# A recurrent attention block with a routed expert layer: VectorE's own reciprocal, two jobs moved from GpSimd to ScalarE, an earlier first set of masked queries, and zero products in the prologue

## The reference

```python
Z1 = xk @ W1_s + b1_s
grad = _ln_fused_l2_bwd(Z1, xv - xk, ln_w, ln_b)
Attn1 = jnp.tril(xq @ xk.swapaxes(-1, -2))
Z1_bar = xq @ W1_s - eta_mb * Attn1 @ grad + b1_bar
W1_new = W1_s - (last_eta * xk).swapaxes(-1, -2) @ grad
out = xq + _ln(Z1_bar, ln_w, ln_b)
```

## Time and profile before

| what | value |
|---|---|
| median of 3 runs | 233.45 us (232.33 to 238.2) |
| the profiled execution, its own time | 233.13 us |
| its span, first to last instruction | 231.2 us, so 1.93 us lie around it |
| VectorE busy | 198.5 us (86%) |
| TensorE busy, matmuls | 194.6 us (84%) |
| GpSimd busy | 154.4 us (67%) |
| ScalarE busy | 115.7 us (50%) |
| mean granted TensorE clock | 0.938 |

### The profile page before, as it was taken

The page is one execution under the profiler, slowest core; times in us unless marked ns, Lnnn a source line. Parts: engine busy times, 40 slices in busy tenths (PEclk is TensorE's granted clock), DMA queues, the critical chain, the costliest instruction groups (busy, mean ns, idle before and its releaser), DMA issues.

```text
span 231.2 us, 5305 instructions
## 1 busy us (share of the span) xinstructions
PE 194.6 (84%) x1893; PEld 154.4 (67%) x1893; DVE 198.5 (86%) x525; ACT 115.7 (50%) x235; POOL 154.4 (67%) x212
## 2 busy tenths in 40 slices
PE   8533999778789979889999985999799599998772
PEld 6313567256678768677968873879588488866551
DVE  2899999999995999999999999999999999206962
ACT  2462179553529063736555755157564556147230
POOL 2314539897779458597687649769999977464234
PEclk9975899979999979999999999799999799988998
DMA  5995200217613000374120044103000300400022
GB/s 166 374 405 169 75 4 0 71 37 157 204 12 91 3 0 10 91 119 65 27 73 3 0 100 135 48 10 91 0 3 10 93 3 0 145 40 0 3 91 91
DMA packets 26000, 17.44 MB, mean 75 GB/s; under 512 B 10552, under 2 KB 24312, under 8 KB 25464
## 3 DMA queue, kind: packets, MB, share of 16 engines
q1 hardware_dynamic: 25464, 16.25, 25.2%
q10 hardware_dynamic: 512, 0.87, 1.2%
HBM read 15.22 MB, written 1.87 MB: 74 GB/s over the span
## 4 chain that ended last, share of the span: by engine, by line
DVE 38%; PE 34%; ACT 8%; POOL 8%; issue 7%; DMA 2%; POOLq 0%; SPq 0%; DVEq 0%; ACTq 0%
PE bank L1174 9%; PE bank L1215 7%; PE bank L1187 5%; PE bank L1133 5%; DVE pr L821 4%; DVE bank L832 4%; DVE pr L880 4%; DVE dW L885 3%; PE bank L1201 3%; POOL hT L355 2%; POOL gw L350 2%; DMA small<-in_small 2%; POOL sgpad L374 2%; PE bank L1251 2%; PE bank L1109 1%
## 5 line engine op out<-in xcount | busy, mean ns | idle before, releaser
L1174 PE MATMUL bank<-xn_hi,gup_hi 128*128 128x256 f32 x128 | 41.0, 320 | 1.6 <-ACT up L583 1.6
L1187 PE MATMUL bank<-down,hT 128*128 128x256 f32 x128 | 34.4, 393 | 4.5 <-ACT G L587 2.5
L350 POOL TENSOR_TENSOR gw<-gate,share 128x256 f32<-128x256 f32 x32 | 23.4, 730 | 21.5 <-ACT gate L582 21.0
L1174 PE MATMUL bank<-xn_hi,gup_lo 128*128 128x256 f32 x128 | 36.9, 288 | 0.0
L1174 PE MATMUL bank<-xn_lo,gup_hi 128*128 128x256 f32 x128 | 36.9, 288 | 0.0
L290 POOL TENSOR_TENSOR A<-A,mask 128x256 f32<-128x256 f32 x32 | 23.5, 735 | 13.2 <-ACT A L565 13.2
L1174 PEld LDWEIGHTS bank<-xn_hi,gup_hi 128*128 128x128 f32 x128 | 25.1, 196 | 7.6 <-issue 4.2
L1187 PEld LDWEIGHTS bank<-down,hT 128*128 128x128 f32 x128 | 22.9, 198 | 7.1 <-issue 2.7
L565 ACT ACTIVATE A<-bank,one 128x256 f32<-128x256 f32 x32 | 15.0, 469 | 23.2 <-PE bank L1133 23.2
L1174 PEld LDWEIGHTS bank<-xn_hi,gup_lo 128*128 128x128 f32 x128 | 25.2, 197 | 0.2
L355 POOL TENSOR_TENSOR hT<-gw,up 128x256 f32<-128x256 f32 x32 | 23.4, 730 | 2.9 <-PE bank L1187 0.5
(11 more groups left out here) (158 smaller groups left out, 436.7 us busy)
## 6 DMA issues: line engine op xcount, KB each, us to landing
wblk<-w_blocks SPq DMA_DIRECT2D x8, 512.0 KB, 4.0
share<-shares SPq DMA_DIRECT2D x8, 512.0 KB, 8.3
sgpad<-in_gup SPq DMA_DIRECT2D x1, 1024.0 KB, 9.6
G<-in_gup SPq DMA_DIRECT2D x1, 1024.0 KB, 11.7
down<-in_down SPq DMA_DIRECT2D x1, 1024.0 KB, 14.2
xkT<-in_x_bt SPq DMA_DIRECT2D x1, 1024.0 KB, 4.8
out<-G SPq DMA_DIRECT2D x4, 256.0 KB, 2.5
wkv<-in_wkv ACTq DMA_DIRECT2D x1, 512.0 KB, 4.2
```

The lines of the kernel that those rows point to most:

```text
L350: pool.tensor_tensor(gw[:, :], gate[:, i % 2, :], share[:, pair % 2, e, :], ALU.mult).then_inc(S_["gw"], 1)
L1174: ins = pe.matmul(bank[4 + i % 2][:, 2 * P * g:2 * P * g + 2 * P], w[:, k, e, NI * g:NI * g + NI].bitcast(F32R), x[:, k, 2 * pair:2 * pair ...
L1187: ins = pe.matmul(bank[7][:, HS * r:HS * r + HS], hT[:, i % 2, P * r:P * r + P], down[:, e, :], start=(e == 0 and r == 0), stop=(e == NE - ...
```

## The change

1. **VectorE and ScalarE, each minibatch.** The sum of squares is taken over 9 columns per token instead of 8; the ninth holds 8*eps, set once. So sxx is 8*(v + eps) with no bias. VectorE takes the reciprocal of sxx itself (16 values, no wait for ScalarE) and multiplies it by ScalarE's square root (16 values) to get the other row. ScalarE's second row (L572) is gone, and its square root has no bias operand. The factor 8 is taken up by constants elsewhere; the last addition to x becomes one operation with a factor 1/8.
2. **Masked queries** go from GpSimd to ScalarE (four `Copy` activations with a per-partition scale): those of group 0 behind the second sigmoid and the sqrt table, of group 1 behind `query_rows(1)`, of group j + 1 behind `step_std(2j+2)` and ahead of the group's remaining slots.
3. **Keys by token** of groups 3 to 7 go from GpSimd to ScalarE, behind `step_std(2j+1)`.
4. **ScalarE's prologue**: the copies of xn's channels (groups 1 to 3) go ahead of `input_std(2)`.
5. **TensorE's prologue**: 2, 7 and 1 zero products.

The core of the diff:

```diff
-        T = sb("T", [P, 5, HD * K])
+        T = sb("T", [P, 4, HD * K])
+        XX = sb("XX", [P, K, HD + 1])
...
-                act.activation(sv[:, 0, :], sxx[:, :], ACT.Sqrt, bias=eps[:, 0:1], scale=1.0 / HD).then_inc(S_["rstd"], 1)
-                act.activation(sv[:, 1, :], sxx[:, :], ACT.Identity, bias=eps[:, 0:1], scale=1.0 / HD).then_inc(S_["rstd"], 1)
+                act.activation(sv[:, :], sxx[:, :], ACT.Sqrt, scale=1.0 / HD).then_inc(S_["rstd"], 1)
...
+            link(v.memset(XX[:, :, HD:], HD * EPS))
...
-                v.tensor_reduce(sxx[:, :], xx, AX.X, ALU.add).then_inc(S_["vrc"], 1)
+                v.tensor_reduce(sxx[:, :], XX[:, :, :], AX.X, ALU.add).then_inc(S_["vrc"], 1)
...
-                v.wait_ge(S_["rstd"], 2 * n + 2)
-                v.reciprocal(rr, sv[:, :, :]).then_inc(chain, 1)
+                v.wait_ge(S_["vrc"], n + 1)
+                v.reciprocal(rr[:, 1, :], sxx[:, :]).then_inc(chain, 1)
+                v.wait_ge(S_["rstd"], n + 1)
+                done(9)
+                v.tensor_tensor(rr[:, 0, :], rr[:, 1, :], sv[:, :], ALU.mult).then_inc(chain, 1)
...
-                v.tensor_tensor(x, x, b3(cs[:, 0, :]), ALU.add).then_inc(S_["sg"], 1)
+                v.scalar_tensor_tensor(out=x, in0=b3(cs[:, 0, :]), scalar=1.0 / HD, in1=x,
+                                       op0=ALU.mult, op1=ALU.add).then_inc(S_["sg"], 1)
...
+            def masked_queries(j):
+
+                act.wait_ge(S_["qchc"], 2 + 2 * (j // 4))
+                if j >= 2:
+                    act.wait_ge(S_["sc"], 4 * (j - 1))
+                for h in range(4):
+                    act.activation(xqm[:, j % 2, :, :, h, :], xqT[:, :, :, GT * j:GT * j + GT], ACT.Copy,
+                                   scale=cmask[:, h:h + 1]).then_inc(S_["queries"], 1)
+
+            def keys_by_token(j):
+
+                act.wait_ge(S_["pair_done"], j)
+                act.copy(KT[:, j % 2, :, 0:HD], KP[:, j % 2, 0:HD, :].rearrange("p c t -> p t c")).then_inc(S_["kts"], 1)
...
-            input_std(2, 4, 8)
             xn_out((2, 4), 2, 1, 4)
+            input_std(2, 4, 8)
...
+            masked_queries(0)
             step_std(2)
...
             query_rows(1)
+            masked_queries(1)
...
+                    if j < NG - 1:
+                        keys_by_token(j + 1)
                     scores_out(j, 2)
...
                     step_std(2 * j + 2)
                 if j == 4:
                     scores_out(j, 4)
+                if j < NG - 1:
+                    masked_queries(j + 1)
                 for i in slots:
                     expert_slot(i)
...
+            zero_products(2)
             pe.wait_ge(S_["wt"], 1)
             target_rows(0, bank[5][:, 0:256]).then_inc(S_["pair0"], 1)
+            zero_products(7)
             xn_channels((2, 4), 1, 4)
+            zero_products(1)
```

More of the change, by code:

```diff
@@ L128, in build @@
         sxx = sb("sxx", [P, K])
-        sv = sb("sv", [P, 2, K])
+        sv = sb("sv", [P, K])
         cs = sb("cs", [P, 2, K])
@@ L327, in bias_targets @@
                 pool.wait_ge(S_["pair_done"] if j else S_["pair0T"], j or 1)
-                if j:
+                if j in (1, 2):
                     pool.tensor_copy(KT[:, j % 2, :, 0:HD], KP[:, j % 2, 0:HD, :].rearrange("p c t -> p t c")).then_inc(S_["kts"], 1)
@@ L331, in bias_targets @@
                 pool.tensor_tensor(q, q, gb[:, :].unsqueeze(1).broadcast_to([P, GT, HD]), ALU.add).then_inc(S_["targets"], 1)
-            def masked_queries(j):
-                pool.wait_ge(S_["qchc"], 2 + 2 * (j // 4))
-                if j >= 2:
-                    pool.wait_ge(S_["sc"], 4 * (j - 1))
-                for h in range(4):
-                    pool.tensor_scalar(xqm[:, j % 2, :, :, h, :], xqT[:, :, :, GT * j:GT * j + GT],
-                                       cmask[:, h:h + 1], 0.0, ALU.mult, ALU.add).then_inc(S_["queries"], 1)
             def hidden_product(i):
@@ L505, in input_std @@
                 if n == 0:
-                    act.wait_ge(S_["dve0"], 3)
+                    act.wait_ge(S_["dve0"], 4)
                 act.activation(std_in[:, first:end], mv[:, first:end, 1], ACT.Sqrt,
@@ L632, in _ @@
             step_std(0)
+            xn_out((2, 4), 2, 1, 4)
             input_std(2, 4, 8)
-            xn_out((2, 4), 2, 1, 4)
             keys_out(0, (0, 1), 0, 4)
@@ L648, in _ @@
             preload_sqrt(1)
+            act.wait_ge(S_["small2"], 16)
+            masked_queries(0)
             step_std(2)
@@ L797, in route_choices @@
                                     mif[:, :, k:k + 1].broadcast_to([P, NF, NE]), ALU.is_equal).then_inc(S_["onehot"], 1)
-            OPS = 17
+            OPS = 18
             def minibatch(j, ring, m, fill, last=False):
@@ L812, in minibatch @@
                 b3 = lambda a: a.unsqueeze(2).broadcast_to([P, K, HD])
-                xs, xx, u, pq, ux = (td(T[:, i, :]) for i in range(5))
+                xs, u, pq, ux = (td(T[:, i, :]) for i in range(4))
                 x = td(x_ps)
@@ L841, in minibatch @@
                 done(3)
-                v.tensor_tensor(xx, x, xs, ALU.mult).then_inc(chain, 1)
+                v.tensor_tensor(XX[:, :, 0:HD], x, xs, ALU.mult).then_inc(chain, 1)
                 done(4)
@@ L845, in minibatch @@
                 done(6)
-                v.tensor_reduce(sxx[:, :], xx, AX.X, ALU.add).then_inc(S_["vrc"], 1)
+                v.tensor_reduce(sxx[:, :], XX[:, :, :], AX.X, ALU.add).then_inc(S_["vrc"], 1)
                 done(7)
-                v.tensor_reduce(S[:, :, :], T[:, 2:5, :].rearrange("p k (t d) -> p k t d", d=HD), AX.X,
+                v.tensor_reduce(S[:, :, :], T[:, 1:4, :].rearrange("p k (t d) -> p k t d", d=HD), AX.X,
                                 ALU.add).then_inc(chain, 1)
                 fill(1)
-                v.wait_ge(S_["rstd"], 2 * n + 2)
-                v.reciprocal(rr, sv[:, :, :]).then_inc(chain, 1)
+                v.wait_ge(S_["vrc"], n + 1)
[3 more added lines that the diff above has]
+                v.tensor_tensor(rr[:, 0, :], rr[:, 1, :], sv[:, :], ALU.mult).then_inc(chain, 1)
                 fill(3)
-                done(9)
+                done(10)
                 v.tensor_tensor(rs[:, :, :], rr, S[:, 1:3, :], ALU.mult).then_inc(chain, 1)
                 v.tensor_tensor(rr, rr, sg_n.unsqueeze(1).broadcast_to([P, 2, K]), ALU.mult).then_inc(chain, 1)
-                done(10)
+                done(11)
                 v.tensor_reduce(S[:, 1, :], rs[:, :, :].rearrange("p k t -> p t k"), AX.X, ALU.add).then_inc(chain, 1)
-                done(11)
+                done(12)
                 v.tensor_tensor(aq, q, b3(rr[:, 0, :]), ALU.mult).then_inc(chain, 1)
-                done(12)
-                v.scalar_tensor_tensor(out=cs[:, :, :], in0=S[:, 0:2, :], scalar=-1.0 / HD,
+                done(13)
+                v.scalar_tensor_tensor(out=cs[:, :, :], in0=S[:, 0:2, :], scalar=-1.0,
                                        in1=rr[:, 1:2, :].broadcast_to([P, 2, K]),
@@ L866, in minibatch @@
                 v.tensor_tensor(sg_td, u, b3(rr[:, 1, :]), ALU.mult).then_inc(chain, 1)
-                done(14)
+                done(15)
                 v.tensor_tensor(x, x, b3(cs[:, 1, :]), ALU.mult).then_inc(chain, 1)
-                done(15)
+                done(16)
                 v.tensor_tensor(h, aq, sg_td, ALU.add).then_inc(chain, 1)
-                done(16)
-                v.tensor_tensor(x, x, b3(cs[:, 0, :]), ALU.add).then_inc(S_["sg"], 1)
                 done(17)
+                v.scalar_tensor_tensor(out=x, in0=b3(cs[:, 0, :]), scalar=1.0 / HD, in1=x,
+                                       op0=ALU.mult, op1=ALU.add).then_inc(S_["sg"], 1)
+                done(18)
                 v.wait_ge(S_["sg"], 4 * n + 1)
@@ L1253, in project, with zero_products @@
                 ins.then_inc(S_["o"], 1)
+            def zero_products(count):
+                for _ in range(count):
+                    pe.matmul(bank[1][:, 0:256], pe_warm[:, 0:P], pe_warm[:, :], start=True, stop=True)
             pe.wait_ge(S_["xn0"], 1)
@@ L1326, in _ @@
                 project(f)
-            def zero_products(count):
-                for _ in range(count):
-                    pe.matmul(bank[1][:, 0:256], pe_warm[:, 0:P], pe_warm[:, :], start=True, stop=True)
             pe.wait_ge(S_["zc"], 8)
```

9 lines of the change are left out of this document (2 added, 7 removed).

## The result

The changed kernel takes 238.55 us (median of 4 runs, 236.19 to 240.52) against 233.03 (4 runs, 232.33 to 238.2): a ratio of 1.0193, 95% interval 1.0134 to 1.0252. It is slower, and outside the range given. The one of 236.19 us was the fastest of the four; the other three left no trace. So the profiles here account for 3.1 of the 5.5 us between the medians.

A forecast was written before the change was run, and what follows sets the result against it. VectorE's recurrence was taken to bound the kernel to n = 14, then the end from ScalarE's G. VectorE's fifteenth sum 1.1 us sooner, G's path 1.3 longer: +0.2, 233.3 us profiled, 233.6 median; range 228.8 to 238.1 (0.88).

The forecast's parts named there:

- the bound of 0.06: VectorE's last addition as a scaled one: taken as 0, at most 0.06 us per step, 0.8 us in the range.
- Rival C: VectorE's reciprocal stays at 0.36 us and the scaled addition costs 0.06 more: 235.1 us, median 235.4; chance 0.15.
- the 2.4 left over: VectorE's wait for ScalarE in n = 4, 2.6 us before, was to remain at about 2.4 us.
- Seven free steps (5 to 11): VectorE's steps n = 5 to 11, with no filled work, gain 0.07 us each, 0.5 us in all.
- the end's uncovered piece: Group 6's masked queries on ScalarE lengthen root of n = 14 to G from 1.81 to 3.11 us: 1.3 us lost.
- The copy of keys: Keys by token on ScalarE, one copy of 0.3 to 0.5 us behind the odd root, hidden by waits: 0.
- The prologue: TensorE's keys of group 1 start almost 3 us sooner, but VectorE is occupied there: 0.
- ScalarE's 28.9 us of waits for VectorE hide that: In groups 1 to 5 the queries delay gates by 1.69 less 0.30 us; ScalarE's waits were to absorb it: 0.
- rival A: ScalarE takes over: its longer queue makes VectorE wait in n = 12, n = 14 and the step behind: 237.8 us; chance 0.13.
- A longer wait before E26: TensorE's lower clock behind its wait at the end: at most about another 1 us, not in the sum.
- B: Rival: VectorE's wait of n = 4 goes altogether, 3.1 us gained, 1.3 lost: 231.3 us, median 231.7; chance 0.15.

The follow-up runs named there:

- f4: The changed kernel itself with no edit, run again on one chip beside three other kernels: 236.81 us, ratio 1.0119.
- e1: The kernel before with part 1 alone (VectorE's own reciprocal, ninth column, scaled addition): 232.99 us, ratio 0.9939.
- e3: The changed kernel with the masked queries back on GpSimd, all else kept: 234.21 us, ratio 1.0035.
- f3: The kernel before with parts 1 and 3 (VectorE's reciprocal, keys by token on ScalarE), nothing else: 232.23 us, ratio 0.9932.
- g1: The kernel before with part 1 and 5 zero products on TensorE ahead of the first group_end: 233.91 us, ratio 0.9995.
- g3: The kernel before with parts 1, 4 and 5; masked queries and keys stay on GpSimd: 234.55 us, ratio 0.9936.
- f2: The changed kernel with 7 zero products on TensorE ahead of group 3's first slot and 13 ahead of E26's down product: 234.5 us, ratio 1.0023.
- g2: The kernel before with part 1, 5 zero products ahead of the first group_end, and n = 4's root ahead of the scores' fourth part: 232.72 us, ratio 0.9951.

## Why the prediction was wrong

**Right: what bounds the kernel, and the lengths on VectorE.** The recurrence paces the kernel to n = 14, and the end begins with G. The groups of VectorE after show the sizes:

```profile
L861 DVE RECIPROCAL bank<-sxx 128x16 f32<-128x16 f32 x16 | 3.9, 243 | 0.0
...
L864 DVE TENSOR_TENSOR bank<-bank,sv 128x16 f32<-128x16 f32 x16 | 2.9, 182 | 5.5 <-ACT sv L573 4.5
...
L883 DVE SCALAR_TENSOR_TENSOR bank<-cs,bank 128x128 f32<-128x128 f32 x16 | 4.6, 290 | 0.0
```

Reciprocal 0.24 (I had 0.25), product 0.18 (0.18), scaled addition 0.290 where the plain one took 0.293 (the value 0, not the bound of 0.06). In n = 7 the products with the factors start at 103.56, the sums at 102.60: 0.96, for 0.97. Rival C falls by these lengths.

Two agreements are less than they look. From the root of n = 3 to that of n = 4 the way is 0.31 shorter (0.3 forecast), and n = 4's wait 2.24 for the 2.4 left over. That is luck: a second profile of the same kernel (f4) has 14.93 us for that way, not 13.72, and a wait of 3.44. And the term "Seven free steps (5 to 11) give 7 x 0.07 = 0.5" was too small. From the root of n = 4 to that of n = 11, e1, e3, f3 and g1 took 72.9 us against 74.27 before, 1.4 less. In n = 6 a gap of 0.27 us ahead of VectorE's product hb is gone too; the rest of the difference is open.

**Right: the end's uncovered piece.** Masked queries 1.69 us for four (1.69), root to G 3.13 (3.11). The copy of keys took 0.63 us, more than the 0.3 to 0.5 of the sum, and cost nothing all the same (f3). The prologue cost nothing, as far as g3 and the equal profiles of e1 and e3 can tell.

**The step that failed: TensorE's clock in group 3, which the sum puts at nothing.** The sum says of groups 1 to 5: "ScalarE's 28.9 us of waits for VectorE hide that, 2.4 us per wait". For the delay alone this was right. In f2 the gate comes 1.31 us later behind its root and the tile 1.32, the root of n = 8 still has 0.94 us of reserve of the 2.79 before, and from n = 4 to n = 14 VectorE takes 106.95 us, 106.80 with the queries on GpSimd (e1). But the gate is also what TensorE waits for, 3.45 us now instead of 0.92. Behind this wait its clock fell (0.74 in 92 to 112, 1.00 before), and the way from gate to tile grew by 2.8 us (11.05 against 8.24). 1.3 us of delay fit into a reserve of 2.79, 1.3 and 2.8 together do not: VectorE waits 2.26 us in n = 8 and 9, where the sum had none. The prediction had the mechanism in its hands: "The new holes before late gates are of that kind" stands under rival A, without a price, and the forecast has 0 for it. An average wait of one engine was set against the delay without asking what the delay does to the engine between.

**The one price that the prediction gave the clock, "A longer wait before E26 costs at most about another 1 us", nearly held.** It was 1.28 at the tile (7,1) and 0.35 from G to the end. It too had no place in the sum.

So the loss has two parts of about the same size. Kernels with part 1 and the queries on GpSimd measure 0.9932 to 0.9951 (e1, f3, g2, g3; e3 and g1 1.0035 and 0.9995), the changed kernel 1.0119 and 1.0193, and with the same delays and the clock held (f2) 1.0023: the hold takes back 1.0 to 1.7%. In the traces 2.2 us are group 3's, where the clock decides, and 1.6 the longer way from the root of n = 14 to G (3.12 against 1.52), pure delay. f2's ratio flatters the clock's share a little, since its second hold also gives back what the kernel before lost behind G (1.6 us at the tile).

The Trainium skill (TensorE: Matmul & The Clock Gate, HAM oscillation) states, for waits on DMA, that where a wait parts each batch of matmuls from the next, every batch starts at the low clock; the prediction cited it and left it out of the sum. The rows behind 3.45 and 6.30 us of waiting agree with it. Those in group 1 of the same execution do not: behind 3.18 us the group's products took 2.18 us, at the full clock.

**Rivals.** A had the sign and nearly the time (237.8), not the place: it put VectorE's waits in n = 12 and 14, where ScalarE has no reserve; they came in n = 8 and 9, and n = 12's root started at 158.23, 0.33 later than before. B's wait of n = 4 did not go.

**What stays open.** Why the clock fell behind a wait of 3.45 us in group 3, and behind one of 3.19 in group 1 of f4 (the group's products took 3.39 us) but not behind the same wait of 3.18 in the changed kernel's first profile; why it fell after short waits in g1; why the last output products are slow in some executions; and what the executions of 237.65 to 240.52 us lost beyond the profiled one. Queries in front of the roots in group 1 and 2 were not tried.
